# Key products of two blocks at once: the middle stage of a spectral attention kernel in turns of two blocks

## The chip, the cores and the metric

The kernel runs on one core of a Trainium2 chip. The metric is the device time of one execution in microseconds (us), from the first to the last instruction of the slowest core; here there is only one. The core has a matrix engine (PE), a vector engine (DVE), a scalar engine (ACT), a general engine (POOL) and a sync engine (SP) that here only issues transfers. Each engine works through its own program in order and waits on semaphores for the others.

## The reference

64 spectra `x` (256 degrees by 257 orders, complex) are turned into rows, then pass one attention layer and one small feed-forward layer:

```
coeff = complex(x) * sqrt_eig;  s = einsum('nlm,mlk->nkm', coeff, pct);  h = irfft(s, n=512)   # (64, 256, 512)
z = layernorm(h);  key = z @ K;  logits = tanh(key @ z.T + bias)
logits -= 10000 outside a band of 12;  scores = softmax(logits * temperature)
h = h + scores @ z
h = h + ffn(layernorm(h))     # 7 small layers, only on rows whose two marks are above 0.5; changes 32 columns
```

Layer norm has no weights, so the kernel applies its scale `rstd` afterwards. `K` and the transform are folded into one matrix `G`, so that keys come from the spectrum of a block and not from its rows. A block is one of the 64 items, 256 rows.

## The kernel before

There are three stages. The first (`stage1_spectrum`) multiplies the coefficients with `pct` and writes the spectra to DRAM; the last 12 groups of orders stay in an SBUF area called `hold` and are read from there for blocks 0 to 3 and stored to DRAM for the others (`store_held`, semaphore `hold_stored`). The middle stage (`stage2_blocks`) does transform, attention and output of all 64 blocks. The last stage runs the feed-forward layer on the marked rows.

Precision comes from splitting: each operand of a product is a high part (`sphi`, `keyhi`, `hhi`, `pThi`, rounded copies by ACT) and a low part (`splo`, `keylo`, `hlo`, `pTlo`, the rest by a subtraction on DVE), and `product3` (L668) issues three matmuls, high by high, high by low, low by high, per pair of 128 by 128 weights. For one block PE does:

- `keys` (L677): 4 output groups `e` of 4 depths of 3 matmuls, so 48 of 256 columns, weights `Ghi`/`Glo`, moving operand the block's spectrum, into two PSUM banks `ps_k`;
- `logits` (L722): 24 matmuls of 256 columns into `ps_l`;
- `probs_T`: 4 transposes of the probabilities into `ps_pT`; `rank`: 2 tiny ones; `inverse_dft`: 16 of 128 columns into `ps_dft`;
- `attend` (L733): 12 matmuls of 512 columns into `ps_av`.

ACT and DVE do the rest of a block: after the logits, DVE scales them (L1308), ACT takes tanh (L1057), DVE adds the band and finds the least (L1207), ACT takes the exponential (L989), PE transposes, ACT and DVE split (L1015, L1239). After `attend`, DVE adds the result to the rows (L1158, "mix"), ACT squares and sums (L953), POOL makes the root, ACT writes the output (L971). For a new block ACT copies the odd part of the transform (L1028), DVE makes the rows (L1274, L1286 to L1291), ACT squares and sums (L1049), and POOL makes `rstd`, which SP sends to DRAM and back as a row (`rrow`).

The stage is a software pipeline. Each engine has a function `slot(i, k, has)` that is its program for one slot, and `slots` (L550) runs i = -1 to 66. In slot i PE does, in this order, `keys(i)`, `probs_T(i-1)`, `rank(i-3)`, `inverse_dft(i+1)`, `logits(i)`, `attend(i-1)`. ACT copies `keyhi` in two halves around `sphi` of block i+1, DVE makes `keylo` likewise. At slot 59 (`LOOP[1]`) SP loads the constants of the last stage; at slot 60 (`WEIGHTS`) ACT and DVE round and split them (L980 to L981, `split_weights`) ahead of everything else of the slot. SP interleaves the stores of `hold` with the `rs` and `rrow` transfers of slots 0, 1 and 2:

```
if isinstance(i, int) and 0 <= i < 3:
    store_held(1 + 2 * i, min(3 + 2 * i, 6))
```

`sphi` and `splo` lie in an area of their own, two blocks deep, and are ready for slot i as soon as block i's spectrum is.

Of the kernel before, what the change touches and what calls it, by code (L numbers as in the profile page):

```python
# [17 lines left out]
P = 128  # L18
# [324 lines left out]
def stage2_blocks(nc, const, ffn_consts, spec, recs, rs, out):  # L343


    with ExitStack() as ctx:
# [16 lines left out]
        sb("early", [P, 10752])  # L363
# [9 lines left out]
        keyhi = place("keyhi", early_at + 38912, [P, CH, NLAT], F32R)  # L373
# [4 lines left out]
        held_at = const.hold_at  # L378
        act_f = place("act_f", held_at, [P, 2, TILES5, 512])
# [8 lines left out]
        y = place("y", held_at + 45568, [P, 512])  # L388

# [4 lines left out]
        keylo = sb("keylo", [P, CH, NLAT], F32R)  # L394
        rrow = sb("rrow", [P, 2, NLAT])
        lsc = sb("lsc", [P, TILES, NLAT])
        th = sb("th", [P, TILES, NLAT])
        lg = sb("lg", [P, TILES, NLAT])
# [33 lines left out]
        hot = sb("hot", [P, 2 * TJ, 16])  # L432
# [97 lines left out]
        FIRST, LAST = -1, NB + 2  # L530
        LOOP = (7, NB - 5)
# [18 lines left out]
        def slots(eng, slot):  # L550
            for i in range(FIRST, LOOP[0]):
                slot(i, i % 4, lambda n: 0 <= n < NB)
            with eng.Fori(LOOP[0], LOOP[1] - 3, 4) as i0:
                for u in range(4):
                    slot(i0 + u, (LOOP[0] + u) % 4, lambda n: True)
            for i in range(LOOP[1], LAST + 1):
                slot(i, i % 4, lambda n: 0 <= n < NB)
# [23 lines left out]
        def _(sp):  # L581
# [43 lines left out]
            def slot(i, k, has):  # L625
                if has(i):
                    sp.wait_ge(pool_rstd1, i + 1)
                    sp.dma_start(rs[i].rearrange("(p t) -> p t", p=P), rstd1[:, k, :]).then_inc(rs_written, 16)
                    wait(sp, dve_scaled, i - 1)
                    sp.wait_ge(rs_written, i * 16 + 16)  # L630
                    sp.dma_start(rrow[:, k % 2], rs[i].unsqueeze(0).to_broadcast([P, NLAT])).then_inc(rrow_loaded[k % 2], 16)
                if isinstance(i, int) and 0 <= i < 3:
                    store_held(1 + 2 * i, min(3 + 2 * i, 6))
                if isinstance(i, int) and i == 2:
                    sp.wait_ge(hold_stored, 16 * HELD)
                    for n in range(2):
                        sp.wait_ge(pe_dft, n * 2 + 2)
                        sp.wait_ge(act_sphi, n + 1)
                        sp.wait_ge(dve_splo, n + 1)
                        load(n + 4, n)  # L640
                if has(i) and has(i + 4) and not (isinstance(i, int) and i < 2):
                    sp.wait_ge(pe_dft, i * 2 + 2)
                    sp.wait_ge(act_sphi, i + 1)
                    sp.wait_ge(dve_splo, i + 1)
                    load(i + 4, k)
                if isinstance(i, int) and 2 <= i < 7:
                    empty_records((0, 1, 5, 9, 13)[i - 2], (1, 5, 9, 13, 16)[i - 2])
                if isinstance(i, int) and i == LOOP[1]:
                    for dst, src in ffn_consts:
                        sp.dma_start(dst, src).then_inc(ffn_loaded, 16)  # L650
                if isinstance(i, int) and i == AHEAD + 3:
                    for r in range(4):
                        sp.wait_ge(rec_sent[r], 32 * ((AHEAD - r + 3) // 4))
                    sp.wait_ge(rec_used, 1)
                    load_records(0, 0)
# [946 lines left out]
```

## Time and profile before

| | us |
|---|---|
| median of 3 runs (lowest to highest) | 1435.57 (1432.6 to 1438.91) |
| the profiled execution's own time | 1430.64 |
| its span, first to last instruction | 1428.6 |
| first stage, to the first matmul of the middle stage | about 325 |
| middle stage, to the last `attend` | about 325 to 1229 |
| last stage | about 1229 to 1428 |

Times in the rows below are microseconds from the start of the span. A timeline row gives start, duration, engine, line, operation, output and inputs, and a count; a bracket gives the idle time before it and who ended it. Matmuls are pipelined, so that a matmul's duration is longer than the distance between two starts; distances between starts are what counts on PE. On DVE and ACT the next instruction starts a little before the end of the one before.

### The profile page before, as it was taken

To read this page: it belongs to the slowest core of one execution; us is meant where nothing else is said; L and a number is where in the kernel's file an instruction comes from. 1 tells how busy PE (TensorE), PEld (TensorE's weight loads), DVE (VectorE), ACT (ScalarE), POOL (GpSimd) and SP (SyncE) were. 2 spreads that over 40 slices of the span, in tenths; PEclk is the share of its full clock that TensorE was granted. 3 is DMA by queue.
4 is the path that set the end of the run, shared out by engine and by line. 5 is a ranking of instruction groups with operands and counts; after the bars stand their busy time and mean duration, and the time that the engine had idled before them with its cause. 6 is when DMAs were issued, how large, how long until landed. Compare 5 with 4: busy or idle time off the path is not lost. (4 is left out here: it accounts for less than half of the span.)

```text
span 1428.6 us, 30500 instructions
## 1 busy us (share of the span) xinstructions
PE 1334.1 (93%) x8813; PEld 1158.9 (81%) x8813; DVE 929.4 (65%) x2026; ACT 899.9 (63%) x1956; POOL 559.5 (39%) x1394
## 2 busy tenths in 40 slices
PE   4999778798999999999999999999999989999994
PEld 3778666588899999999999999999999989545551
DVE  1232222235777878878788887888878878767772
ACT  1223222234677777777777777777777777867772
POOL 0000000000355555555555555555555546732222
PEclk8999999999999999999999999999999999999997
DMA  8999999994653433434334343343434332100000
GB/s 346 424 425 424 425 425 425 425 376 146 192 130 92 94 79 96 86 83 90 79 98 85 82 86 82 99 83 83 85 82 100 82 93 59 50 12 9 9 4 5
DMA packets 88315, 219.69 MB, mean 154 GB/s; under 512 B 20784, under 2 KB 33724, under 8 KB 75900
## 3 DMA queue, kind: packets, MB, share of 16 engines
q1 hardware_dynamic: 78728, 190.33, 42.8%
q10 hardware_dynamic: 4164, 27.27, 4.5%
q0 software_dynamic: 5376, 1.52, 0.6%
q8 instruction: 23, 0.38, 0.1%
q14 instruction: 24, 0.20, 0.1%
HBM read 147.77 MB, written 72.68 MB: 154 GB/s over the span
## 5 line engine op out<-in xcount | busy, mean ns | idle before, releaser
L674 PE MATMUL ps_k<-sphi,Glo 128*128 128x256 f32 x1024 | 292.2, 285 | 0.0
L673 PE MATMUL ps_k<-splo,Ghi 128*128 128x256 f32 x1024 | 291.0, 284 | 0.0
L672 PE MATMUL ps_k<-sphi,Ghi 128*128 128x256 f32 x1024 | 288.6, 282 | 0.0
L261 PE MATMUL s1b<-pg,cg 128*128 128x256 f32 x1024 | 240.5, 393 | 48.0 <-DVE cg L231 46.8
L261 PEld LDWEIGHTS s1b<-pg,cg 128*128 128x128 f32 x1024 | 198.0, 196 | 93.0 <-issue 33.9
L231 DVE TENSOR_TENSOR cg<-xg,se 128x1024 f32<-128x1024 f32 x63 | 77.2, 1225 | 221.5 <-DMA pg<-in_pct_dram 211.0
L1442 POOL TENSOR_SCALAR ve<-var 128x2 f32<-128x2 f32 x64 | 13.9, 217 | 479.8 <-ACT squares L1049 479.7
L672 PEld LDWEIGHTS ps_k<-sphi,Ghi 128*128 128x128 f32 x1024 | 194.7, 190 | 2.4
L673 PEld LDWEIGHTS ps_k<-splo,Ghi 128*128 128x128 f32 x1024 | 193.1, 189 | 2.7
L674 PEld LDWEIGHTS ps_k<-sphi,Glo 128*128 128x128 f32 x1024 | 193.7, 189 | 0.0
L316 ACT COPY stage<-s1b 128x512 f32<-128x512 f32 x104 | 60.7, 585 | 169.5 <-PE s1b L261 165.2
L1430 POOL DMA_INDIRECT recs<-rec,idx x128 | 136.9, 1069 | 54.6 <-issue 54.3
L672 PE MATMUL ps_l<-sphi,keyhi 128*128 128x256 f32 x512 | 150.9, 295 | 5.6 <-DVE keylo L1230 2.4
L673 PE MATMUL ps_l<-splo,keyhi 128*128 128x256 f32 x512 | 145.5, 284 | 0.0
L674 PE MATMUL ps_l<-sphi,keylo 128*128 128x256 f32 x512 | 145.4, 284 | 0.0
L708 PE MATMUL ps_dft<-dft,xt 128*128 128x129 f32 x1008 | 129.4, 282 | 0.0
L708 PEld LDWEIGHTS ps_dft<-dft,xt 128*128 128x128 f32 x1008 | 119.0, 194 | 0.0
L1049 ACT ACTIVATE squares<-h 128x512 bf16<-128x512 f32 x128 | 79.7, 624 | 56.6 <-DVE h L1291 56.6
L672 PEld LDWEIGHTS ps_l<-sphi,keyhi 128*128 128x128 f32 x512 | 98.7, 193 | 6.5 <-issue 5.3
L672 PE MATMUL ps_av<-hhi,pThi 128*128 128x512 f32 x256 | 100.5, 393 | 1.3 <-issue 1.3
L1218 DVE TENSOR_TENSOR keylo<-ps_k,keyhi 128x512 fp32r<-128x512 f32 x64 | 44.3, 692 | 86.8 <-ACT keyhi L999 86.8
L673 PE MATMUL ps_av<-hlo,pThi 128*128 128x512 f32 x256 | 100.4, 392 | 0.0
(175 smaller groups left out, 3181.0 us busy)
## 6 DMA issues: line engine op xcount, KB each, us to landing
pg<-in_pct_dram SPq DMA_DIRECT2D x63, 1024.0 KB, 25.7
out_dram<-o SPq DMA_DIRECT2D x64, 512.0 KB, 2.8
xg<-in_xs_dram SPq DMA_DIRECT2D x63, 512.0 KB, 24.2
xt<-spec SPq DMA_DIRECT2D x60, 512.0 KB, 5.2
spec<-stage ACTq DMA_DIRECT2D x52, 512.0 KB, 8.1
rrow<-rs SPq DMA_DIRECT2D x64, 128.0 KB, 4.6
spec<-hold SPq DMA_DIRECT2D x12, 480.0 KB, 5.2
recs<-rec SPq DMA_DIRECT2D x16, 160.0 KB, 5.6
```

The lines of the kernel that those rows point to most:

```text
L231: nc.vector.tensor_tensor(cg[:, b % SETS], xg[:, b], se_view(g), ALU.mult).then_inc(scaled, 1)
L261: last = nc.tensor.matmul(bank[at * PARTS + part][:, m % 2, :], cg[:, b % SETS, m * 2 + h, :], pg[:, b, m * 2 + h, :], start=(h == 0), sto ...
L316: nc.scalar.copy(to, bank[at * PARTS + j][:, :, :]).then_inc(copied, 1)
L672: nc.tensor.matmul(out_ap, whi, mhi, start=(j == 0), stop=False)
L673: nc.tensor.matmul(out_ap, whi, mlo, start=False, stop=False)
L674: last = nc.tensor.matmul(out_ap, wlo, mhi, start=False, stop=(j == n - 1))
L708: last = nc.tensor.matmul(ps_dft[t][:, cols[0]:cols[1]], x[:, src, t * P:(t + 1) * P], dft[:, cols[0]:cols[1]], start=True, stop=True)
L1049: nc.scalar.activation(squares[:, 0, t], h[:, k1, t], ACT.Square, scale=1.0 / math.sqrt(NLON), accum_out=var1[:, k1 % 2, t:t + 1]).then_in ...
L1218: nc.vector.tensor_tensor(keylo[:, 0:2, :].rearrange("p e w -> p (e w)"), ps_k[0][:, :], keyhi[:, 0:2, :].bitcast(F32).rearrange("p e w -> ...
L1430: nc.gpsimd.indirect_dma_start(out=recs[:, :], out_offset=bass.IndirectOffsetOnAxis(ap=idx[:, r4, t:t + 1], axis=0), in_=rec[:, r4, t, :], ...
L1442: nc.gpsimd.tensor_scalar(ve[:, 0, :], var1[:, k % 2, :], EPS, None, ALU.add).then_inc(pool_ve, 1)
```

## The change

The middle stage goes in turns of two blocks, a and a+1. `keys` now takes the spectra of both as one moving operand of 512 columns, so that a pair of blocks has 48 matmuls of 512 columns where it had 96 of 256. A group `e` fills one PSUM bank for both blocks, so that group 2 needs the bank of group 0 and group 3 that of group 1; the copies to `keyhi` and `keylo` are four per turn, one for each group. The spectra of a pair lie side by side, and there are two pairs; the second (`sphi1`, `splo1`) lies in the area `hold`. `lsc`, `th` and `lg` are dropped: the scaled logits, tanh, the band sum and the exponential are all written in place in `pr`. The program of each engine is rewritten for a turn. `exponentials` is L989, `squares1` L1049, `squares2` L953, `outputs` L971, `tangent` L1057, `odd_part` L1028, `rows_high` L1033, `spectrum_high` L1005; on DVE `least` is L1207, `mix` L1158, `rows_made` L1286 to L1291, `tail` the three small steps before the record, `even_odd` L1274, `scale_logits` L1308.

Places and bounds, and what SP does:

```diff
-        sphi = place("sphi", early_at + 16384, [P, 2, CH, NLAT], F32R)
-        splo = place("splo", early_at + 24576, [P, 2, CH, NLAT], F32R)
...
+        sphi = [place("sphi0", early_at + 16384, [P, CH, 2, NLAT], F32R),
+                place("sphi1", held_at, [P, CH, 2, NLAT], F32R)]
+        splo = [place("splo0", early_at + 24576, [P, CH, 2, NLAT], F32R),
+                place("splo1", held_at + 8192, [P, CH, 2, NLAT], F32R)]
...
-        LOOP = (7, NB - 5)
+        FIRST, LAST = -2, NB
+        LOOP = (6, NB - 6)
...
+                first = isinstance(a, int) and a == 0
...
+                if first:
+                    store_held(1, 3)
+                if has(a + 1):
+                    root_row(a + 1, r + 1)
+                if first:
+                    store_held(3, 6)
                     sp.wait_ge(hold_stored, 16 * HELD)
...
+                if has(a) and has(a + 4):
+                    load_behind(a, r)
...
+                if isinstance(a, int) and a == LOOP[1]:
                     for dst, src in ffn_consts:
                         sp.dma_start(dst, src).then_inc(ffn_loaded, 16)
...
+                if has(a + 2):
+                    root_row(a + 2, (r + 2) % 4)
```

PE, the keys and the order of a turn:

```diff
+            def keys(a, r):
+                pe.wait_ge(act_sphi, a + 2)
+                pe.wait_ge(dve_splo, a + 2)
+                for e in range(CH):
+                    wait(pe, act_keyhi, a * 2 + (e - 1 if e > 1 else 0))
+                    wait(pe, dve_keylo, a * 2 + (e - 1 if e > 1 else 0))
+                    product3(ps_k[e % 2][:, :],
+                             [(Ghi[:, d, e * P:(e + 1) * P], Glo[:, d, e * P:(e + 1) * P],
+                               sphi[r // 2][:, d].rearrange("p b w -> p (b w)"),
+                               splo[r // 2][:, d].rearrange("p b w -> p (b w)")) for d in range(CH)]).then_inc(pe_key, 1)
...
+                if has(a):
+                    keys(a, r)
...
+                if has(a - 1):
+                    probs_T(a - 1)
+                if has(a - 3):
+                    rank(a - 3, r + 1, a)
+                if has(a + 2):
+                    inverse_dft(a + 2, (r + 2) % 4)
+                if has(a):
+                    logits(a, r, a - 2)
+                if has(a - 1):
+                    attend(a - 1, (r + 3) % 4)
+                if has(a - 2) and not ending:
+                    rank(a - 2, r, a + 1)
+                if has(a + 3):
+                    inverse_dft(a + 3, (r + 3) % 4)
...
                     features_T(0)
+                if has(a):
+                    probs_T(a)
+                if has(a + 1):
+                    logits(a + 1, r + 1, a - 1)
+                if has(a):
+                    attend(a, r)
```

ACT, the high parts and the order of a turn:

```diff
+            def spectrum_high(n, r):
+                wait_spectrum(act, n, r)
+                if isinstance(n, int) and n == 2:
                     act.wait_ge(hold_stored, 16 * HELD)
...
+                    for q in (1, 3):
+                        act.wait_ge(x_loaded[q], 48)
+                wait(act, pe_logit, (n if r % 2 == 0 else n - 1) - 2)
+                nc.scalar.copy(sphi[r // 2][:, :, r % 2, :], spectrum_of(n, r)).then_inc(act_sphi, 1)
...
+                if isinstance(a, int) and a == WEIGHTS:
+                    weights()
+                if has(a - 1):
+                    exponentials(a - 1, (r + 3) % 4)
...
+                    squares2(a - 2, r % 2)
+                if has(a + 1):
+                    squares1(a + 1, r + 1)
+                if has(a):
+                    key_high(a, 0)
+                if has(a - 3) and not ending:
+                    outputs(a - 3, r + 1)
+                if has(a):
+                    key_high(a, 1)
+                if has(a + 2) and not start:
+                    spectrum_high(a + 2, (r + 2) % 4)
+                if has(a - 1) and not ending:
+                    rows_high(a - 1, (r + 3) % 4)
+                if has(a):
+                    key_high(a, 2)
+                if has(a + 3) and not start:
+                    spectrum_high(a + 3, (r + 3) % 4)
+                if has(a):
+                    key_high(a, 3)
+                if has(a - 1) and not ending:
+                    probs_high(a - 1, (r + 3) % 4)
+                if has(a - 3):
+                    places(a - 3, (r + 1) % 2)
+                if has(a + 2):
+                    odd_part(a + 2)
+                if has(a):
+                    rows_high(a, r)
...
+                    outputs(a - 2, r)
+                if has(a):
+                    tangent(a, r)
+                    exponentials(a, r)
+                if has(a + 2) and start:
+                    spectrum_high(a + 2, (r + 2) % 4)
+                    spectrum_high(a + 3, (r + 3) % 4)
+                if has(a - 2) and not ending:
+                    places(a - 2, r % 2)
+                if has(a + 3):
+                    odd_part(a + 3)
+                if isinstance(a, int) and a == NB - 2:
+                    round_in(0)
+                if has(a):
+                    probs_high(a, r)
+                if has(a - 1) and not ending:
+                    squares2(a - 1, (r + 1) % 2)
+                if has(a + 2):
+                    squares1(a + 2, (r + 2) % 4)
+                if has(a + 1):
+                    tangent(a + 1, r + 1)
```

DVE, the order of a turn:

```diff
+                if isinstance(a, int) and a == WEIGHTS:
+                    weights()
+                if has(a - 1):
+                    least(a - 1, (r + 3) % 4)
+                if has(a - 2):
+                    mix(a - 2, (r + 2) % 4)
+                if has(a + 1):
+                    rows_made(a + 1, r + 1)
+                if has(a):
+                    key_low(a, 0)
+                if has(a - 3):
+                    tail(a - 3, (r + 1) % 4)
+                if has(a):
+                    key_low(a, 1)
+                if has(a - 2) and not ending:
+                    tail(a - 2, (r + 2) % 4)
+                if has(a + 2) and not begin:
+                    spectrum_low(a + 2, (r + 2) % 4)
+                if has(a):
+                    key_low(a, 2)
+                if has(a - 1) and not ending:
+                    rows_low(a - 1, (r + 3) % 4)
+                if has(a):
+                    key_low(a, 3)
+                if has(a - 1):
+                    probs_low(a - 1, (r + 3) % 4)
...
+                if has(a + 2):
+                    even_odd(a + 2)
+                if has(a + 3) and not begin:
+                    spectrum_low(a + 3, (r + 3) % 4)
+                if has(a):
+                    scale_logits(a, r)
+                    least(a, r)
+                if has(a - 1) and not ending:
+                    mix(a - 1, (r + 3) % 4)
+                if has(a):
+                    rows_low(a, r)
+                if has(a + 2) and begin:
+                    spectrum_low(a + 2, (r + 2) % 4)
+                if has(a):
+                    probs_low(a, r)
+                if has(a + 2) and begin:
+                    spectrum_low(a + 3, (r + 3) % 4)
+                if has(a + 2):
+                    rows_made(a + 2, (r + 2) % 4)
+                if has(a + 1):
+                    scale_logits(a + 1, r + 1)
+                if has(a + 3):
+                    even_odd(a + 3)
+                if isinstance(a, int) and a == NB - 2:
+                    rows_low(a + 1, r + 1)
+                if ending:
+                    begin_step()
```

POOL does in a turn `root2(a-2)`, `root1(a+1)`, the marks, the record and the sending of block a-3, those of block a-2, `root2(a-1)`, `root1(a+2)`.

## Rows read from the trace of the kernel before

**Rows 1.** The page, its first part: busy time of each engine

```profile
PE 1334.1 (93%) x8813; PEld 1158.9 (81%) x8813; DVE 929.4 (65%) x2026; ACT 899.9 (63%) x1956; POOL 559.5 (39%) x1394
```

**Rows 2.** Windows, 600 to 900 us: busy time, instructions, clock, DMA

```profile
600.00:900.00 300.00, 300.00 (x2311) 288.84 (x2311) 244.60 (x566) 235.24 (x545) 172.00 (x456) 1.00 0.39 88
```

**Rows 3.** Timeline of PE, 800 to 815 us, where the product changes

```profile
800.82 0.40 PE L672 MATMUL ps_av<-hhi,pThi 128*128 128x512 f32 x1
...
803.57 0.29 PE L672 MATMUL ps_k<-sphi,Ghi 128*128 128x256 f32 x1
...
809.34 0.60 PE L696 MATMUL ps_pT<-ident,pr 128*128 128x128 f32 x4
809.78 0.17 PE L718 MATMUL ps_l<-mask,trib 128*128 128x3 bf16 x1
...
811.62 0.37 PE L672 MATMUL ps_l<-sphi,keyhi 128*128 128x256 f32 x1
...
814.58 0.40 PE L672 MATMUL ps_av<-hhi,pThi 128*128 128x512 f32 x1
```

**Rows 4.** Timeline of ACT, 803 to 816 us

```profile
803.43 1.09 ACT L1057 ACTIVATE th<-lsc,bias,rstd 128x256 f32<-128x256 f32 x2 [0.39 <-DVE lsc L1308]
...
806.14 0.63 ACT L953 ACTIVATE squares<-h 128x512 bf16<-128x512 f32 x1 [0.28 <-DVE h L1158]
...
807.39 0.56 ACT L999 CAST keyhi<-ps_k 128x512 fp32r<-128x512 f32 x1
...
810.02 0.84 ACT L1015 ACTIVATE pThi<-ps_pT,rstd 128x256 fp32r<-128x256 f32 x2
...
815.46 0.63 ACT L1049 ACTIVATE squares<-h 128x512 bf16<-128x512 f32 x1 [0.75 <-DVE h L1291]
```

**Rows 5.** Timeline of DVE, 804 to 815 us

```profile
804.16 0.48 DVE L1207 CUSTOM_DVE_ANT_0 lg<-th,band,ntemp 128x256 f32<-128x256 f32 x1 [0.77 <-issue]
...
805.28 1.41 DVE L1158 SCALAR_TENSOR_TENSOR h<-ps_av,rsum,h 128x512 f32<-128x512 f32 x2
808.05 0.69 DVE L1218 TENSOR_TENSOR keylo<-ps_k,keyhi 128x512 fp32r<-128x512 f32 x1 [1.37 <-ACT keyhi L999]
...
810.97 0.88 DVE L1239 SCALAR_TENSOR_TENSOR pTlo<-ps_pT,rstd,pThi 128x256 fp32r<-128x256 f32 x2
811.76 0.47 DVE L1175 TENSOR_SCALAR x<-h,rstd 128x128 f32<-128x128 f32 x2
...
814.07 0.68 DVE L1286 TENSOR_TENSOR h<-eo 128x508 f32<-128x508 f32 x1
```

**Rows 6.** Timeline, 349 to 351 us: PE starts again after DVE

```profile
349.45 0.68 DVE L1230 TENSOR_TENSOR keylo<-ps_k,keyhi 128x512 fp32r<-128x512 f32 x1
...
350.23 0.36 PE L672 MATMUL ps_l<-sphi,keyhi 128*128 128x256 f32 x1 [0.88 <-issue]
```

**Rows 7.** Timeline of SP's queue, 340 to 374 us: the stores of hold

```profile
340.97 5.56 SPq L599 DMA_DIRECT2D spec<-hold  x4
...
354.48 4.49 SPq L599 DMA_DIRECT2D spec<-hold  x4
...
366.69 0.88 SPq L599 DMA_DIRECT2D spec<-hold  x2
372.46 1.44 SPq L584 DMA_DIRECT2D xt<-spec  x3
```

**Rows 8.** Timeline, 1165 to 1176 us: the weights' slot, on DVE and PE

```profile
1165.73 0.68 DVE L1128 TENSOR_TENSOR W1r<-W1f,W1h 64x512 f32<-64x512 f32 x1 [4.58 <-ACT Whi L981]
...
1169.53 0.41 DVE L1207 CUSTOM_DVE_ANT_0 lg<-th,band,ntemp 128x256 f32<-128x256 f32 x1
...
1171.21 1.11 PE L696 MATMUL ps_pT<-ident,pr 128*128 128x128 f32 x4 [3.95 <-ACT pr L989]
...
1172.22 3.77 PE L708 MATMUL ps_dft<-dft,xt 128*128 128x129 f32 x16
```

**Rows 9.** Timeline of PE, 1226 us: the last block's attend

```profile
1226.38 0.47 PE L672 MATMUL ps_av<-hhi,pThi 128*128 128x512 f32 x1 [1.27 <-issue]
```

More of the change, by code:

```diff
@@ L662, in _ @@
+            turns(nc.sync, turn)
+            for n in (NB - 2, NB - 1):
+                store_out(n, n % 4)
             for r in range(4):
@@ L837, in body @@
                 for L in range(2, LAYERS):
-                    layer(s, L, between=(lambda: rank(NB - 1, (NB - 1) % 4)) if opening and L == 2 else None)
+                    layer(s, L, between=(lambda: rank(NB - 1, (NB - 1) % 4, NB)) if opening and L == 2 else None)
                     if L == LAYERS - 2 and not opening:
@@ new lines, in probs_high, with odd_part @@
+            def probs_high(n, r):
+                act.wait_ge(pe_pT, n + 1)
+                wait(act, pe_av, n * 2)
+                for t in range(TILES):
+                    nc.scalar.activation(pThi[:, t, :], ps_pT[:, t, :], ACT.Copy,
+                                         scale=rstd1[:, r, t:t + 1]).then_inc(act_pThi, 1)
+            def odd_part(n):
+                for t in range(TILES):
+                    act.wait_ge(pe_dft, n * 2 + t + 1)
+                    wait(act, dve_eo, (n - 1) * 4 + 2 * t + 2)
+                    nc.scalar.copy(od[:, t, :], ps_dft[t][:, HALF:NLON]).then_inc(act_od, 1)
@@ new lines, in rows_high, with squares1 @@
+            def rows_high(n, r):
+                act.wait_ge(dve_h, n * 3 + 3)
+                wait(act, pe_av, (n - 1) * 2)
+                nc.scalar.copy(hhi[:, r % 2], h[:, r]).then_inc(act_hhi, 1)
+            def squares1(n, r):
+                act.wait_ge(dve_h, n * 3 + 3)
+                wait(act, pool_rstd1, n - 1)
+                wait(act, act_var1, n * 2)
+                for t in range(TILES):
+                    nc.scalar.activation(squares[:, 0, t], h[:, r, t], ACT.Square, scale=1.0 / math.sqrt(NLON),
+                                         accum_out=var1[:, r % 2, t:t + 1]).then_inc(act_var1, 1)
@@ new lines, in weights, with least @@
+            def weights():
+                dve.wait_ge(hold_stored, 16 * HELD)
+                split_weights()
+                nc.vector.memset(feat[:, :, :], 0.0).then_inc(start, 1)
+                nc.vector.memset(res[:, :, :], 0.0).then_inc(rec_used, 1)
+            def least(n, r):
+                wait(dve, act_exp, n * 2)
+                for t in range(TILES):
+                    dve.wait_ge(act_tanh, n * 2 + t + 1)
+                    settled(dve)
+                    nc.vector.tensor_tensor_reduce(out=pr[:, t, :], in0=pr[:, t, :], in1=band[:, t, :],
+                                                   scale=ntemp[:, 0:1], scalar=HIGHEST, op0=ALU.add, op1=ALU.min,
+                                                   accum_out=nmx[:, r % 2, t:t + 1]).then_inc(dve_min, 1)
@@ new lines, in mix, with key_low @@
+            def mix(n, r):
+                sums(n, r % 2)
+                for t in range(TILES):
+                    mix_tile(n, (r + 2) % 4, t)
+            def key_low(a, e):
+                wait(dve, pe_logit, a)
+                dve.wait_ge(act_keyhi, a * 2 + e + 1)
+                nc.vector.tensor_tensor(
+                    keylo[:, e].rearrange("p b w -> p (b w)"), ps_k[e % 2][:, :],
+                    keyhi[:, e].bitcast(F32).rearrange("p b w -> p (b w)"), ALU.subtract).then_inc(dve_keylo, 1)
```

502 lines of the change are left out of this document (206 added, 296 removed).

## The prediction

> **What bounds the kernel now.** I read the page first: PE is busy 93% of the span [rows 1], but a matmul's duration says little, so the windows come next. From 600 to 900 us PE has no idle time at all and holds the full clock of 2.4 GHz, while DVE works 244.6 of 300 us and ACT 235.2 [rows 2]; the transfers take 39% of their engines. The middle stage is therefore set by PE's issue rate, and any edit must be priced by the distance between two matmul starts. The timeline of PE gives it: `keys` runs from 803.57 to 809.34, 5.77 us for 48 matmuls, so 120.2 ns for 256 columns; `attend` from 800.82 to 803.57, 2.75 us for 12, so 229.2 ns for 512 columns [rows 3]. The rest: four transposes 0.44, rank and transform 1.84, logits 2.96, attend 2.75. A block is 5.77 + 0.44 + 1.84 + 2.96 + 2.75 = 13.76 us, a pair 27.52.
>
> **The gain on PE.** A pair's keys become 48 x 229.2 ns = 11.00 us instead of 11.54: 0.54 us per turn, 16.7 over 31 turns, if PE stays dense. The bounds of the price: 227 ns (the smallest distance that rounding of the starts allows) and 240.4 (nothing gained, two times 256 columns). I take 229.2, because `attend` has the same shape, type and weights of 128 columns.
>
> On this point the Trainium skill (TensorE: Matmul & The Clock Gate, "Back-to-back issue gap") speaks against the change: start to start is N / 2.4 + 2.5 ns at the full clock, so 109.2 for 256 columns and 215.8 for 512, a gain of 2.6 ns per pair of matmuls and not 11.2, which would be 0.12 us per turn. The rows show 120.2 and 229.2, both larger than the rule, so I go by the rows.
>
> **Does PE stay dense?** Here the rewritten order decides. Group 2 of the keys needs the bank of group 0, so PE waits there for `key_low(a, 0)`. Before, no product of the keys waited for a copy of the same keys. Call P the moment at which `logits(a+1)` of the turn starts, behind `probs_T(a)`. PE reaches group 2 of the next turn 2.96 (logits) + 2.75 (attend) + 5.50 (groups 0 and 1) = 11.21 us after P. ACT and DVE, in their new order, must do a chain without a gap in the same time; each step is the distance between two starts in the rows of before:
>
> - transposes' end to `probs_high`: 810.02 against 809.34 + 0.60, and PE goes on at 809.78, so P + 0.20 (0.24 in the row, in which ACT comes out of a copy) [rows 3, 4]
> - `probs_high` to `probs_low` 0.95, `probs_low` to the next step of DVE, now `rows_made(a+2)`, 0.79 [rows 4, 5]
> - `rows_made` to `squares1(a+2)` 815.46 - 814.07 = 1.39 [rows 4, 5]
> - `squares1` to the next step, now `tangent(a+1)`: 1.24, by the like pair 806.14 to 807.39 [rows 4]; the scaled logits are there earlier, so that squares stand ahead of tanh
> - tanh to `least(a+1)` 0.73, `least` to `mix(a)` 1.12 [rows 4, 5]
> - `mix` to `rows_made(a+3)`: 1.33, its 1.41 less the overlap of 0.08 to 0.09 that 810.97 + 0.88 against 811.76 shows [rows 5]
> - `rows_made` to `squares1(a+3)` 1.39, `squares1` to `key_high(0)` 1.24 [rows 4, 5]
> - `key_high` to `key_low` 0.66, `key_low` 0.69 [rows 4, 5], and PE 0.10 later (349.45 + 0.68 to 350.23) [rows 6]
>
> The sum is 11.83, so PE arrives 0.62 us early, and its first matmul after a wait costs some 0.08 more (a matmul of 0.36 where 0.28 is usual) [rows 6]. The turn is then 15.75 (P back from group 2: 5.50 + 0.44 + 1.84 + 2.96 + 2.75 + 1.82 + 0.44) + 11.83 + 0.08 = 27.66 us, 0.14 more than the pair of before. Only half of the cheaper matmuls lie on this loop. ACT and DVE are no busier than before; what has changed is that squares of two new blocks and one tanh, least and mix stand in a row ahead of the copy that PE needs. Bounds: each of the 13 steps is read to 0.01 to 0.05, so the wait is 0.3 to 1.0; below 0 the price is -0.54 per turn. Behind the waiting PE stands its whole program. I went through the other waits of a turn in the same way, placing each engine's list on its own timeline; these are estimates: `key_low(1)` is done 1.0 us before group 3 needs it, `key_low(3)` 0.6 before `logits(a)`, `probs_T(a)` finds its exponential 1.2 early, POOL is ready with `root2(a-1)` 5 us early. The in-place tiles change no order, and SP's transfers keep their count. 30 turns, from the one at a = 2 to that at 62: +4.2 us.
>
> **The opening.** `sphi1` lies in `hold`, so `spectrum_high(2)` waits until all of `hold` is stored, and on ACT it stands ahead of `odd_part(3)` and `probs_high(0)`; `attend(0)` waits for those. Before, only SP waited for the stores. When are they done? The first group of four starts at 340.97 and the next at 354.48; the last two take 366.69 to 372.46, 5.77 us [rows 7]. In the new order the remaining six go together behind the row of block 1. Two more pairs at 3.0 to 4.3 each (a group of four less a round trip of some 3, less 5.77) make 13.0 for six. The start shifts little: block 0's rows now wait behind block 1's spectrum on ACT; 0 to 2 us, I take 0.6. Done: 354.48 + 0.6 + 13.0 = 368.1. Then on ACT two spectra of 0.95, odd part 0.55, `probs_high(0)`, and `probs_low(0)` 0.95 later: 371.5. From there DVE does 0.79, `splo` 1.14, and from `rows_made(2)` on the chain above (1.39 + 1.24 + 0.73 + 1.12 + 1.33 + 1.39 + 1.24 + 0.66 + 0.69 + 0.10 = 9.89): group 2 of turn 2 starts at 371.5 + 11.9 = 383.4. PE idles from about 358.5 (logits of block 1) to 372.5, and then runs `attend(0)` at 1.2 GHz, which the same chain hides. Bounds for the group's start: 376 (stores at the queue's best pace) to 388.
>
> **The weights' turn.** At 60 they still stand ahead of everything. The load no longer holds ACT up, since it is issued a turn of 27.7 us ahead. ACT needs some 1.8 for the two copies and DVE 3.80 (1165.73 to 1169.53) [rows 8]; `least(59)` shifts by 5.9, all of it behind a chain that is late already. PE idles 6.5 us and then runs at half the clock: that cost 0.51 in the transposes and 1.93 in the transform of before [rows 3, 8]. 5.9 + 2.4 = 8.3, where before lost 3.95 + 2.4 + 0.3 = 6.7.
>
> **The end.** From the turn at 62 (whose groups 0 and 1 end when group 2 starts, so its origin is 5.5 earlier): keys 11.0, transposes and rank 0.49, logits 2.96, attend 2.75, features 0.8, transposes 0.45, logits 2.96: 21.4. Then scale 0.9, tanh and `rows_high` 2.0, `rows_low` 1.1, `least` 0.6, exponential 1.2, transposes 0.5, split 2.1: `attend(63)` starts 29.9 after the origin.
>
> **The sum.** 383.4 + 0.1 + 30 x 27.66 = 1213.3; + 8.3 = 1221.6; - 5.5 + 29.9 = 1246.0 for `attend(63)`, which starts at 1226.4 before [rows 9]. The last stage is untouched. +19.6 us: +4.2 pace, +1.6 weights, about -1 the end, and the rest, near 15, the opening. The profiled execution took 1430.64 us, so 1450.2; it lies 4.9 under the median of the runs shown, so for the median 1455.
>
> **Rivals.**
>
> - *PE stays dense* (the other side). Place: group 2 of each turn. If one of the 13 steps is shorter than its row, or ACT and DVE have slack that I don't see, the turn is 26.98 and the 30 turns give -16.2 in place of +4.2: 1455 - 20.4 = 1435, no change. It decides for faster when the wait is gone and the opening costs under 8 us in place of 15: 1420 to 1428. For it speaks that DVE and ACT work only 82% and 78% of the time [rows 2]; against it, that the chain is strictly serial across both.
> - *The opening costs little.* The stores land by 360 us and PE goes on: some -10, so 1445 with the wait. Against it: the six stores alone cannot start before 354.5 [rows 7].
> - *The product of 512 columns saves nothing*, 240.4 ns: 24 matmuls on the loop, +0.27 per turn, 1463. By the rule of the Trainium skill named above it would be +0.21 per turn, 1461.
> - *More waits*: `key_low(3)` has 0.6 us of slack, and any further step in the turn that costs over 1 us puts 30 us on the whole: 1466 to 1490.
>
> **How the numbers follow.** Half for the forecast, its own range 1446 to 1463. The dense PE 0.24, split over same (0.11) and faster (0.13); the cheap opening 0.10, half of it within the bound; no saving 0.06; more waits 0.10. A change under 0.5%, 7 us, can't be told from none. Range 1432 to 1466: it leaves out the fast part of the dense case and the worse waits. Faster 0.13, same 0.17, slower 0.70.
>
> **What would show it.** In the profile of the changed kernel: keys of 512 columns 229 ns apart; PE idle 0.6 us once in each turn, ahead of `ps_k` and ended by DVE's `keylo`; turns of 27.7 us; PE idle 12 to 14 us near 360 and ACT's `sphi` waiting for `hold`; an idle of some 6.5 us at turn 60. The forecast is wrong if PE shows no idle at group 2 or if `attend(0)` starts before 365 us.

## The result and the profile after

The changed kernel takes 1477.37 us in the median of 4 runs (1476.65 to 1477.86) where the kernel before took 1435.19 beside it: a ratio of 1.029 [1.027, 1.032], 42 us slower. The forecast was 1455, the range ended at 1466. The direction and the place of the loss were right, its size was about half of what came. The profiled execution took 1477.86 us, its span 1476.1.

The page of the changed kernel, its first part and one line of its groups:

```profile
PE 1334.3 (90%) x7277; PEld 1072.1 (73%) x7277; DVE 933.8 (63%) x2026; ACT 899.2 (61%) x1956; POOL 601.4 (41%) x1394
...
L694 PE MATMUL ps_k<-sphi,Ghi 128*128 128x512 f32 x512 | 206.1, 403 | 29.6 <-DVE keylo L1305 29.6
```

1536 matmuls fewer than in [rows 1], and PE's busy time the same; new is an idle time of 29.6 us ahead of `ps_k`, 6.3 of it in the turn of the weights and the rest in 29 short waits. The windows of the same stretch as in [rows 2]:

```profile
600.00:900.00 300.00, 290.86 (x1728) 251.13 (x1727) 239.62 (x556) 229.23 (x533) 185.35 (x449) 1.00 0.33 80
```

PE is no longer dense: 9.1 us idle in 300. DVE and ACT did less in that stretch than before (239.6 and 229.2 against 244.6 and 235.2), so they had room; the clock stayed at its upper level. PE's timeline shows where the idle lies, always ahead of group 2 of the keys:

```profile
724.19 0.47 PE L694 MATMUL ps_k<-sphi,Ghi 128*128 128x512 f32 x1 [0.96 <-DVE keylo L1305]
...
729.84 0.60 PE L717 MATMUL ps_pT<-ident,pr 128*128 128x128 f32 x4
...
740.11 0.36 PE L694 MATMUL ps_l<-sphi,keyhi 128*128 128x256 f32 x1
...
752.24 0.47 PE L694 MATMUL ps_k<-sphi,Ghi 128*128 128x512 f32 x1 [0.68 <-DVE keylo L1305]
...
780.57 0.47 PE L694 MATMUL ps_k<-sphi,Ghi 128*128 128x512 f32 x1 [0.96 <-DVE keylo L1305]
```

Read as distances: 752.24 - 724.19 = 28.05 us for one turn, 780.57 - 752.24 = 28.33 for the next, and so on in alternation through the loop. Before it was 27.52 for the same two blocks, the forecast was 27.66. The idle is named by the wait that the prediction named.

From 740.11, the point P of the prediction, the chain on ACT and DVE can be followed to 752.24. ACT:

```profile
740.03 0.37 ACT L1052 COPY od<-ps_dft 128x256 f32<-128x256 f32 x1 [0.52 <-PE ps_dft L729]
740.39 0.84 ACT L1044 ACTIVATE pThi<-ps_pT,rstd 128x256 fp32r<-128x256 f32 x2
...
743.69 0.63 ACT L1066 ACTIVATE squares<-h 128x512 bf16<-128x512 f32 x1 [1.23 <-DVE h L1343]
...
744.94 1.08 ACT L1074 ACTIVATE pr<-pr,bias,rstd 128x256 f32<-128x256 f32 x2
...
749.49 0.63 ACT L1066 ACTIVATE squares<-h 128x512 bf16<-128x512 f32 x1 [0.51 <-DVE h L1343]
...
750.74 0.57 ACT L1027 CAST keyhi<-ps_k 128x512 fp32r<-128x512 f32 x1
```

and DVE:

```profile
741.34 0.88 DVE L1321 SCALAR_TENSOR_TENSOR pTlo<-ps_pT,rstd,pThi 128x256 fp32r<-128x256 f32 x2 [0.85 <-ACT pThi L1044]
742.13 0.68 DVE L1339 TENSOR_TENSOR h<-eo 128x508 f32<-128x508 f32 x1
...
743.32 0.33 DVE L1343 COPY h<-eo 128x8 f32<-128x8 f32 x1
...
745.66 0.48 DVE L1291 CUSTOM_DVE_ANT_0 pr<-pr,band,ntemp 128x256 f32<-128x256 f32 x1 [0.26 <-ACT pr L1074]
...
746.77 1.41 DVE L1243 SCALAR_TENSOR_TENSOR h<-ps_av,rsum,h 128x512 f32<-128x512 f32 x2
748.09 0.68 DVE L1339 TENSOR_TENSOR h<-eo 128x508 f32<-128x508 f32 x1
...
749.28 0.17 DVE L1343 COPY h<-eo 128x8 f32<-128x8 f32 x1
...
751.40 0.69 DVE L1305 TENSOR_TENSOR keylo<-ps_k,keyhi 128x512 fp32r<-128x512 f32 x1 [1.95 <-ACT keyhi L1027]
```

It is the forecast chain, link by link. Ten of the 13 steps differ by 0.02 us or less; three are longer. P to `probs_high` is 0.28 and not 0.20, since the copy `od` at 740.03 stands ahead of it; `rows_made` to `squares1(a+2)` is 1.56 and not 1.39 (the copy of 743.32 takes 0.33, like 27 of the 31 that have `scale_logits`, a reader of PSUM, directly behind them; the one of 749.28 takes 0.17, like all the others); `key_low` to PE is 0.84 and not 0.79. The chain has 12.13 us in place of 11.83.

The opening, with SP's queue, ACT and PE:

```profile
358.08 7.93 SPq L601 DMA_DIRECT2D spec<-hold  x6
...
370.35 1.99 ACT L1037 CAST sphi<-xt 128x1024 fp32r<-128x1024 f32 x2 [11.74 <-issue]
...
374.63 0.77 PE L694 MATMUL ps_av<-hhi,pThi 128*128 128x512 f32 x1 [12.44 <-ACT pThi L1044]
```

PE stands idle for 12.4 us (12 to 14 were forecast) and goes on when `hold` is stored. What comes next is not as forecast. The windows row of `attend(0)` (span, busy time of each engine, granted clock), then the `keylo` that group 2 of turn 2 needs, and the start of that group:

```profile
374.63:379.89 5.26, 5.26 (x12) 4.10 (x13) 5.17 (x14) 2.68 (x7) 0.94 (x2) 0.50 0.11 43
```

```profile
384.68 0.69 DVE L1305 TENSOR_TENSOR keylo<-ps_k,keyhi 128x512 fp32r<-128x512 f32 x1 [1.94 <-ACT keyhi L1027]
...
385.84 0.39 PE L694 MATMUL ps_k<-sphi,Ghi 128*128 128x512 f32 x1
```

`attend(0)` takes 5.26 us at a granted clock of 0.50, 1.2 GHz, where 2.75 are usual, and PE starts group 2 without an idle, some 0.5 us after `keylo` is done. Here the chain did not hide the slow clock; PE itself came last.

### The profile page after: what moved, and what is told of

Read it like the earlier page. It is cut to its first block, busy times and chain, and to the rows that moved or that the text cites. A ratio compares the mean times of both kernels' runs of the same rounds, so it can differ in the third digit from the quotient of the medians.

```text
span 1476.1 us, 27759 instructions
## 1 busy us (share of the span) xinstructions
PE 1334.3 (90%) x7277; PEld 1072.1 (73%) x7277; DVE 933.8 (63%) x2026; ACT 899.2 (61%) x1956; POOL 601.4 (41%) x1394
## 3 DMA queue, kind: packets, MB, share of 16 engines
q1 hardware_dynamic: 78728, 190.33, 39.7%
## 4 chain that ended last, share of the span: by engine, by line
PE 43%; DVE 12%; ACT 9%; issue 8%; POOL 1%; DMA 1%; ACTq 1%; SPq 1%; DVEq 0%; another core or an unknown queue 0%; POOLq 0%
PE ps_dft L729 8%; PE ps_k L694 5%; PE ps_k L695 4%; PE ps_k L696 4%; ACT squares L1066 3%; DVE h L1339 2%; DVE h L1341 2%; ACT pr L1074 2%; PE ps_l L694 2%; PE ps_l L696 2%; PE ps_l L695 2%; DVE h L1243 2%; PE ps_av L694 2%; PE ps_av L695 2%; PE ps_av L696 2%
## 5 line engine op out<-in xcount | busy, mean ns | idle before, releaser
L694 PE MATMUL ps_k<-sphi,Ghi 128*128 128x512 f32 x512 | 206.1, 403 | 29.6 <-DVE keylo L1305 29.6
L231 DVE TENSOR_TENSOR cg<-xg,se 128x1024 f32<-128x1024 f32 x63 | 77.2, 1226 | 225.9 <-DMA pg<-in_pct_dram 209.9
L695 PE MATMUL ps_k<-splo,Ghi 128*128 128x512 f32 x512 | 203.1, 397 | 0.0
L696 PE MATMUL ps_k<-sphi,Glo 128*128 128x512 f32 x512 | 202.8, 396 | 0.0
L1580 POOL TENSOR_SCALAR ve<-var 128x2 f32<-128x2 f32 x64 | 14.7, 229 | 383.8 <-ACT squares L1066 381.0
L1570 POOL DMA_INDIRECT recs<-rec,idx x128 | 151.9, 1187 | 46.2 <-issue 44.5
L1305 DVE TENSOR_TENSOR keylo<-ps_k,keyhi 128x512 fp32r<-128x512 f32 x128 | 88.3, 690 | 97.4 <-ACT keyhi L1027 94.6
L694 PEld LDWEIGHTS ps_k<-sphi,Ghi 128*128 128x128 f32 x512 | 97.2, 190 | 63.2 <-ACT keyhi L1027 41.8
L696 PEld LDWEIGHTS ps_k<-sphi,Glo 128*128 128x128 f32 x512 | 97.1, 190 | 23.1
L694 PE MATMUL ps_av<-hhi,pThi 128*128 128x512 f32 x256 | 102.3, 400 | 12.4 <-ACT pThi L1044 12.4
L695 PEld LDWEIGHTS ps_k<-splo,Ghi 128*128 128x128 f32 x512 | 97.4, 190 | 21.4
L1027 ACT CAST keyhi<-ps_k 128x512 fp32r<-128x512 f32 x128 | 74.0, 578 | 55.8 <-PE ps_k L696 54.2
```

Of the source, the lines that this page charges most:

```text
L231: nc.vector.tensor_tensor(cg[:, b % SETS], xg[:, b], se_view(g), ALU.mult).then_inc(scaled, 1)
L694: nc.tensor.matmul(out_ap, whi, mhi, start=(j == 0), stop=False)
L695: nc.tensor.matmul(out_ap, whi, mlo, start=False, stop=False)
L696: last = nc.tensor.matmul(out_ap, wlo, mhi, start=False, stop=(j == n - 1))
L1027: nc.scalar.copy(keyhi[:, e].rearrange("p b w -> p (b w)"), ps_k[e % 2][:, :]).then_inc(act_keyhi, 1)
L1305: nc.vector.tensor_tensor(keylo[:, e].rearrange("p b w -> p (b w)"), ps_k[e % 2][:, :], keyhi[:, e].bitcast(F32).rearrange("p b w -> p (b ...
```

## The experiments

All times of a run are read beside the kernel before on the same chip, so the ratio counts; medians of different runs are not to be compared. "Middle" is the distance on PE's timeline from the transposes that end the first stage to `attend(63)`; it leaves out the first stage, which differs by up to 3.7 us from one profiled run to the next, and the last. "Turn" is the distance of the same matmul in two turns of the loop.

| run | ratio to before | median us | middle us | turn us |
| --- | --- | --- | --- | --- |
| before | 1 | 1435.2 | 901.1 | 27.52 |
| changed | 1.029 [1.027, 1.032] | 1477.4 | 936.7 | 28.05 / 28.33 |
| e1 key copy first | 1.006 [1.004, 1.008] | 1437.9 | 904.8 | 27.12 |
| e2 products of 256 | 1.032 [1.030, 1.033] | 1474.4 | 939.7 | 28.17 / 28.45 |
| e3 spectra last in turn 0 | 1.026 [1.024, 1.027] | 1466.5 | 932.1 | 28.05 / 28.33 |
| e4 tanh before squares | 1.018 [1.016, 1.020] | 1455.7 | 923.7 | 27.61 / 27.80 |
| f0 changed, again | 1.029 [1.027, 1.032] | 1474.5 | 936.6 | 28.05 / 28.33 |
| f1 first stores only | 1.024 [1.021, 1.026] | 1466.6 | 925.6 | 28.05 / 28.33 |
| f2 e1 with products of 256 | 1.015 [1.012, 1.019] | 1454.7 | 914.1 | 27.51 |
| f3 e1 + f1 + weights | 0.995 [0.993, 0.997] | 1425.8 | 884.5 | 27.12 |
| g1 f3 + end order | 0.991 [0.989, 0.992] | 1422.2 | 885.5 | 27.12 |
| g2 loop of four turns | one run | 1499.1 | 960.0 | 28.05 / 33 to 34 |
| g3 weights in gaps | 1.022 [1.020, 1.025] | 1468.0 | 930.0 | 28.05 / 28.33 |
| g4 outputs before key copy | one run | 1548.4 | 1010.8 | 29.47 / 31.0 to 31.4 |

**f0: the changed kernel once more**, as a measure for the later runs.

> The changed kernel itself, once more, on the chip of the runs beside it, as their measure: 1.029 of the kernel before, all theories alike.

It repeats to 0.0003 of the ratio, and its middle to 0.1 us.

**e1: the first key copy ahead of the squares.** In ACT's turn:

```
-                if has(a + 1):
-                    squares1(a + 1, r + 1)
                 if has(a):
                     key_high(a, 0)
+                if has(a + 1):
+                    squares1(a + 1, r + 1)
```

> ACT copies the first key group (key_high(a,0)) ahead of squares1(a+1) instead of behind it. Serial chain theory: the steps rows_made, squares1 (1.40) and the copy's 1.25 no longer stand in a row; the copy starts some 1.7 us earlier, DVE is idle then, all waits of PE at group 2 (0.68 and 0.96 in turn) go, the turn falls from 28.19 to about 27.1, 28 turns and the one at the end give -30: 1447 us (1443 to 1452). Rival, ACT and DVE are simply too loaded in the new order: another wait takes the place (group 3, key_low(3) ahead of logits(a), or the exponentials) and the time stays within 7 us of 1477. Rival, contention: the single instructions stay longer than before and half of the gain comes, 1462.

Windows of this run:

```profile
600.00:900.00 300.00, 300.00 (x1812) 263.01 (x1811) 247.99 (x574) 236.90 (x554) 192.31 (x468) 1.00 0.34 88
```

PE is dense again, with one swap of two lines; the turn is 27.12 us and the middle 31.9 us shorter. No other wait took the place, and DVE and ACT work more per us than before the change without holding anyone up. Both rivals fall: it was order, not load. The turn gives PE's own price too: 27.12 without any idle, against 27.52 before, so the product of 512 columns is worth 0.40 us per turn. In the same rows 48 of them take 11.15 us, 232.3 ns each, 3 ns more than those of `attend`.

**e2 and f2: products of 256 columns, with the wait and without it.**

```
-                    product3(ps_k[e % 2][:, :],
...
+                    for q in range(2):
+                        last = product3(ps_k[e % 2][:, q * NLAT:(q + 1) * NLAT],
+                                        [(Ghi[:, d, e * P:(e + 1) * P], Glo[:, d, e * P:(e + 1) * P],
+                                          sphi[r // 2][:, d, q], splo[r // 2][:, d, q]) for d in range(CH)])
```

> The keys of a pair as 96 products of 256 columns again, order of all engines as in the changed kernel. Chain theory: only groups 2 and 3 lie on the loop that sets the turn (from group 2 to logits(a+1)); 24 products of 231 ns become 48 of 120.2, +0.2 to 0.25 per turn, so +6 to +7 us: 1484. Groups 0 and 1 grow into the wait of PE, which falls by 0.2 to 0.25. Rival, PE's issue sets the whole turn: +0.45 per turn, +14: 1491. Rival, the product of 512 columns saved nothing: 1477 and unchanged distance between the starts per column.

> The first key copy ahead of the squares (as in the run before of that kind, 1.006 of the kernel before), with products of 256 columns. There PE is dense, so this prices the product alone on the path: by the distances read (48 x 120.2 = 5.77 per block against 24 x 231 = 5.55) +0.43 us per turn of two blocks, turn 27.55 instead of 27.125, +13 us, 1.015 of the kernel before. Rival, the product of 512 columns saves nothing: 1.006, turn 27.1. Rival, ACT or DVE bind first: turn unchanged too, but with an idle of PE to be seen.

Under the wait, undoing the product costs 0.12 us per turn and 3 us in the middle, and PE's waits fall from 0.96 and 0.68 to 0.77 and 0.49: groups 0 and 1 grow into the wait. That is half of what was expected. The restart behind a wait costs 0.08 with 512 columns (the first distance is 0.31 where 0.23 is usual). With 256 the first distance is longer too, 0.19 where 0.12 is usual, but from group 2 to the transposes it is still 5.77 us, 48 x 120.2 ns, as without a wait. Without the wait, in f2 against e1, the same edit costs 0.38 per turn and 0.009 of the time, 13 us (9.3 in the middle), about as expected. The interval of e2's ratio and that of the changed kernel overlap, so its 3 us rest on the traces alone.

**e3 and f1: two ways around the wait for `hold`.** e3 moves the spectra of blocks 2 and 3 to the end of the first turn on ACT (as below) and likewise on DVE:

```
-                if has(a + 2) and start:
-                    spectrum_high(a + 2, (r + 2) % 4)
-                    spectrum_high(a + 3, (r + 3) % 4)
...
                 if has(a + 1):
                     tangent(a + 1, r + 1)
+                if has(a + 2) and start:
+                    spectrum_high(a + 2, (r + 2) % 4)
+                    spectrum_high(a + 3, (r + 3) % 4)
```

f1 leaves the order and cuts the wait down to the four stores that read what `sphi1` and `splo1` overwrite:

```
-                                     const.hold[c * NB + 4:c * NB + NB, 8 * j:8 * j + 8, :]).then_inc(hold_stored, 16)
+                                     const.hold[c * NB + 4:c * NB + NB, 8 * j:8 * j + 8, :]).then_inc(hold_first if j < 2 else hold_stored, 16)
...
-                    act.wait_ge(hold_stored, 16 * HELD)
+                    act.wait_ge(hold_first, 64)
```

> In the first turn the spectra of blocks 2 and 3, which need the stored hold, come last on ACT and DVE; probs_high(0), squares1(2) and tangent(1) go ahead of them. Theory: attend(0) starts near 362 instead of 374.6, keys(2) near 374 instead of 377.4, but least(1) to key_low(2,0) stand behind the second spectrum_low (about 373.6): group 2 of turn 2 at about 380.3 instead of 385.4, -5 us: 1472. Rival, the wait for the stores costs nothing of its own since the chain binds anyway: 1477 (0 to -1.5). Rival, the whole idle of 12.4 us is to be had by order alone: 1465.

> The changed kernel, but spectrum_high(2) waits only for the four stores that read the part of hold under sphi1 and splo1 (rows 0 to 15 of its 48), by a semaphore of their own, and not for all twelve. Theory of the prediction (the opening's loss is this wait): ACT goes on near 358 instead of 370, attend(0) starts near 362.5 instead of 374.6, group 2 of turn 2 near 373.5 instead of 385.4, and 12 us are gained: 0.8% below the changed kernel. Rival: the load of blocks 4 and 5 behind the last store (near 370) then holds back the transform of block 4 and half of the gain is lost, -6. Rival: nothing, since the chain of that turn binds anyway, 0.

e3 gained 4.6 us in the middle, f1 11.0, both close to the first theory. The timeline of f1:

```profile
358.53 1.98 ACT L1039 CAST sphi<-xt 128x1024 fp32r<-128x1024 f32 x2
...
362.80 0.47 PE L696 MATMUL ps_av<-hhi,pThi 128*128 128x512 f32 x1 [0.59 <-issue]
...
373.68 0.47 PE L696 MATMUL ps_k<-sphi,Ghi 128*128 128x512 f32 x1 [2.30 <-DVE keylo L1307]
```

The idle of 12.4 us ahead of `attend(0)` is 0.6, and 2.3 come back at group 2, where the chain is late. Behind that wait the granted clock of the next 5.6 us is 0.70. By the ratio the gain is 8 us and not 11, and the interval of each ratio, some 4 us to either side, allows both.

**e4: tanh ahead of the squares**, on ACT.

```
+                if has(a + 1):
+                    tangent(a + 1, r + 1)
                 if has(a + 2):
                     squares1(a + 2, (r + 2) % 4)
-                if has(a + 1):
-                    tangent(a + 1, r + 1)
```

> ACT does tangent(a+1) ahead of squares1(a+2). Chain theory: tanh can start when the logits are scaled (744.0 + 0.08) instead of behind the squares (744.94), so the chain is 0.86 shorter; the waits of 0.68 and 0.96 shrink to 0 and 0.1, turn 27.35 in the mean, -23 us: 1454 (1450 to 1460). Rival, squares1(a+2) later by 1.1 makes the row of block a+2 late on POOL and SP, and scale_logits(a+2) waits: 1477 or slower. Rival, the chain is not what PE waits for: 1477.

A miss in size: 13 us of 23. ACT does start the tanh 0.82 us earlier after `probs_high` (3.73 against 4.55), but DVE, its next link, is not free:

```profile
761.73 1.41 DVE L1331 TENSOR_TENSOR eo<-ps_dft,od 128x256 f32<-128x256 f32 x4
763.05 0.48 DVE L1291 CUSTOM_DVE_ANT_0 pr<-pr,band,ntemp 128x256 f32<-128x256 f32 x1
```

`even_odd(a+3)`, so far hidden, now stands on the chain, and `least` starts 1.20 behind the tanh in place of 0.72. About half of the 0.82 is left: the turns are 0.44 and 0.53 shorter, 27.61 and 27.80.

**g4: the chain made longer by a known step, with the same work.** On ACT:

```
+                if has(a - 3) and not ending:
+                    outputs(a - 3, r + 1)
                 if has(a):
                     key_high(a, 0)
-                if has(a - 3) and not ending:
-                    outputs(a - 3, r + 1)
```

> The changed kernel with outputs(a-3), 1.42 us of ACT, ahead of key_high(a,0) instead of behind it: the same work, the chain longer by 1.42. Serial chain theory: each of the 28 turns 1.40 longer (28.19 to 29.6), the wait of PE at group 2 of 0.8 becomes 2.2, +40 us: some 1515. Rival, the load of ACT and DVE sets the turn: the same work in another order, 1474 as before.

The load theory falls a second time. Each fourth turn is 29.47 us, 1.42 above 28.05, as the chain has it. The others cost 1.5 to 1.9 more than that, 0.28 of it the loop's end in every second turn; the rest I had not foreseen. PE's timeline and its windows (span, busy time of each engine, granted clock):

```profile
687.19 0.77 PE L694 MATMUL ps_k<-sphi,Ghi 128*128 128x512 f32 x1 [2.37 <-DVE keylo L1305]
...
718.07 0.47 PE L694 MATMUL ps_k<-sphi,Ghi 128*128 128x512 f32 x1 [2.09 <-DVE keylo L1305]
```

```profile
687.20:692.80 5.60, 5.60 (x18) 4.52 (x19) 4.19 (x13) 2.62 (x4) 3.87 (x15) 0.72 0.42 10
...
718.10:723.70 5.60, 5.60 (x24) 4.51 (x25) 5.46 (x14) 2.94 (x4) 4.53 (x14) 1.00 0.39 14
...
778.80:784.40 5.60, 5.56 (x17) 4.47 (x18) 4.14 (x13) 2.43 (x4) 3.75 (x15) 0.70 0.14 8
```

Behind the idle of 2.37 us PE ran a part of the next 5.6 us at 1.2 GHz (18 matmuls where there are 24 at the full clock); behind the one of 2.09 at 718 it did not, and behind one of the same length at 778.8 it did. Of the nine such waits in a row from 625 to 871 us, seven were followed by 5.6 us at 0.70 to 0.73 and two by 1.00; such a stretch has 6 or 7 matmuls of 0.23 us fewer, which is the 1.4 to 1.7 us. In the changed kernel, whose waits are below 1 us, the clock is 1.00 from 600 to 900 us.

**g2: four turns in the loop's body.** It asks why the turns alternate.

```
-        LOOP = (6, NB - 6)
+        LOOP = (6, NB - 10)
...
-            with eng.Fori(LOOP[0], LOOP[1] - 3, 4) as a0:
-                for u in (0, 2):
+            with eng.Fori(LOOP[0], LOOP[1] - 7, 8) as a0:
+                for u in (0, 2, 4, 6):
```

> The changed kernel with four turns in the loop's body (six passes over turns 6 to 52) in place of two. The turns alternate 28.05 and 28.33 there. Theory: the 0.28 is the loop's end on ACT and DVE, which falls between the squares or tanh of one turn and the exponentials and least of the next, in the middle of the chain: then three turns in a row take 28.05 and each fourth 28.33, the turns written out (54 to 58) 28.05; in all some -2 us. Rival: it comes from the parity of the pair (bank, buffer, queue): the alternation stays.

Three turns in a row take 28.05 and so do those written out behind the loop, so the 0.28 belongs to the loop's end, not to the parity of a bank or a queue. But each fourth turn takes 33 to 34 us, and the run is 25 us slower. The page's list of queues for the changed kernel has

```profile
q14 instruction: 25, 0.20, 0.1%
```

and for this run, with, under it, a line of its waits (us in all, times, longest):

```profile
q14 instruction: 109, 0.89, 0.4%
```

```profile
DVE pr L1291 <- issue: 21.0, 25, 2.0
```

Two of DVE's first instructions of a pass (`least`) wait 1.6 to 2.0 us each for nothing that the program orders, and four times as many instruction packets are moved. The likeliest reading is that the longer body is fetched again in each pass; that the fetch is the cause was not tried by itself.

**g3, f3 and g1: the weights, and all together.** g3 takes only the weights out of the way: `W1h` in turn 58, `Whi` in 60, and DVE's four operations in gaps of turns 60 and 62:

```
                 if has(a - 1) and not ending:
                     squares2(a - 1, (r + 1) % 2)
+                if isinstance(a, int) and a == WEIGHTS - 2:
+                    weights()
+                if isinstance(a, int) and a == WEIGHTS:
+                    weights2()
...
+                if isinstance(a, int) and a == WEIGHTS:
+                    weights()
+                if isinstance(a, int) and a == WEIGHTS + 2:
+                    split_weights3()
                 if has(a):
                     key_low(a, 1)
```

f3 joins this with e1 and f1. g1 changes the last turn as well, first on ACT, then on DVE:

```
                 if ending:
+                    outputs(a - 3, r + 1)
                     relu(0, 0, range(0, 2))
-                    outputs(a - 3, r + 1)
...
+                if ending:
+                    scaled_part(a - 3, (r + 1) % 2)
+                    rows_low(a - 1, (r + 3) % 4)
...
-                if isinstance(a, int) and a == NB - 2:
-                    rows_low(a + 1, r + 1)
```

> The changed kernel with the weights of the last stage in four pieces in the gaps of turns 58, 60 and 62, and nothing else. By the prediction's term (8.3 us for weights ahead of turn 60) and the 7.6 us that its turn is longer than the others: -7 to -8 us, 1.024 of the kernel before, PE's idle of 6.3 there back to 0.7. Rival: the pieces delay the chain, which is late in each of these turns, by their 3.8 us: -3 to -4.

> The first key copy ahead of the squares, the wait for the first four stores only, and the weights of the last stage rounded in four pieces over turns 58, 60 and 62, each in a gap of ACT or DVE, instead of all ahead of turn 60. Against the key copy alone (1.006 of the kernel before, 1437.9 us): -12 for the opening, -6 for the weights (PE idle of 4.4 and half-clock of some 2.4 gone, 0.8 lost to pieces longer than their gap): 0.993 to 0.995 of the kernel before, faster by 0.5 to 0.7%. Rival: a gain in one place is given back in another wait (the two are not additive), 1.000.

> The kernel with the key copy first, the wait for the first stores only and the weights in gaps (0.995 of the kernel before), and with its last turn reordered: least(63) ahead of rows_low(63), x2 of block 61 behind it and ahead of mix(62), outputs(61) ahead of the first relu. Theory: the last records are set out by POOL in one row from the mark of block 61 on, and the last stage's second step waits for them; POOL starts some 2 us earlier and no longer waits 2.8 us for the outputs of 61: -4 us, 0.992. attend(63) starts near 1206.3 where it was 1209.1. Rival: relu later by 1.4 us makes the first step of the last stage the bound, and nothing is gained: 0.995.

g3: middle 6.6 us shorter (7 to 8 expected), and PE's idle of 6.3 us there is 0.5. f3: 20.3 shorter than e1 (18 expected), so the two edits add up, and the kernel is 0.5% faster than before the change. g1: `attend(63)` did not come earlier (the middle is 1.0 longer: it waits 1.7 us for `pTlo`), but POOL sends its last records 29.7 us behind it in place of 32.7; 0.991 [0.989, 0.992], the fastest kernel of the study. f3 and g1 differ by 0.004 in ratio, 6 us, with intervals that do not meet, but only by 1.4 us in their traces behind the first stage, so how much the end order brings stays open.

## Why the prediction was wrong in size

Measured against its own sum: `attend(63)` was forecast at 1246.0 and started at 1265.1, and behind it 8.8 us were added where the prediction had none.

- *First stage*, +3.0. Its last transposes start at 328.34, and at 325.32 before. That part of the program is the same; f0, the same kernel, has 326.44.
- *Opening*, -0.7. Group 2 of turn 2 started at 385.8, 3.0 of that from the stage before; forecast 383.5. The stores were done at 370.3, so 367.3 without the shift (368.1 forecast). That the sum fits so well is in part luck: the slow `attend(0)`, which the chain was to hide, set this start, and the early stores made up for it. e3 and f1 show the wait to be the cause, and f1 that four of the twelve stores were enough to wait for.
- *The turn*, +14.7: the step that failed. "27.66 us, 0.14 more than the pair of before" was 28.19 in the mean over the 28 turns from 385.8 to 1175.0. Of the 0.53, the chain's three longer steps are 0.30; PE's own way back from group 2 to P is 15.93 in place of 15.83, mostly since keys of 512 columns cost 232.3 ns and not the 229.2 of `attend`; and 0.13 is the loop's end, 0.28 in every second turn of the loop, which the prediction did not have at all. The mechanism was right: e1 takes it away by order alone, g4 lengthens it by what is put into it. What made the size treacherous is that a wait is the small difference of two long sums, 11.83 and 11.21: 0.3 us read short in 13 steps of one is half as much again on the wait, times 28. The prediction's own bound for the wait, 1.0 us, would have given 30 x 0.38 = 11 us more, 1466: the range ended where this one term ended and had no room for the others.
- *Gain on PE*, 0.40 per turn and not 0.54, for the same 3 ns; it mattered little here, because most of it fell into the wait (e2); it counted in full once the wait was gone (f2). By the formula of the Trainium skill (TensorE: Matmul & The Clock Gate, "Back-to-back issue gap"), which that section gives for a single matmul, the gain would be 0.12 per turn. It had the direction of the miss; its two distances, 109.2 and 215.8 ns, are below both that were measured, 120.2 and 232.3 ns.
- *Weights*, +0.1: two turns took 63.7 us, forecast 63.6. Two errors meet here: the plain turn was longer than forecast, and the weights cost 7.6 us above it and not 8.3. g3 gives 6.6 of the 7.6 back.
- *The end*, +1.9 up to `attend(63)`: a wait of 2.3 us for the exponential and one of 1.9 us for POOL that the count of PE's work left out.
- *Last stage*, "untouched", +8.8. 4.1 are real: POOL sends its last records later behind `attend(63)`, since it waits for `outputs(61)`, which ACT does behind the first relu:

```profile
1268.54 0.24 POOL L1521 COPY rec<-o 128x64 f32<-128x64 f32 x1 [2.77 <-ACT o L1003]
```

  The other 4.7 are one stall in the last stage (a step of 39.7 us where its neighbours take 35.0) that nine of the fourteen profiled executions have, none of e1 to e4 and all of f0 to g4, and that the one of the kernel before happened not to have. The forecast had added 4.9 us for the distance of the profiled run from its median. By its size that covers the stall, which nothing in the working knew; so against 1455 the miss is 22 us, though the terms above miss by 28.

Two small slips in the working change nothing: the rows allow 2.74 / 12 = 228 ns as the smallest distance and not 227, and the terms of the end add up to 29.8 and not 29.9.

The rivals: *PE stays dense* needed an order that the change did not have; with it (e1) the time is 1.006 of before, 1444 on the scale of the forecast where the rival said 1435, the rest being PE's smaller gain and the last stage. *The product saves nothing* is refuted by f2 against e1, *the opening costs little* by `attend(0)` at 374.6. *More waits* had the right size for the wrong reason: `key_low(3)` held.

## What to carry to other kernels

When work is paired, ask what now stands in one row ahead of the first copy that frees a bank; a swap of two steps of one engine was worth 32 us here, and the product itself about 12. A wait forecast as a difference of two sums wants a range as wide as the reading error of all its steps, plus what the loop's end costs on each engine. Where a tile takes over space that is still being stored, wait for the stores of that space, not for all.

## What the runs showed that I had not expected

- A loop's end costs about 0.28 us on a chain that crosses it; twice the body did away with half of these and cost 5 to 6 us per pass instead, with 109 instruction packets in place of 25 (g2).
- Waits of 2.1 to 2.4 us, once a turn, brought the granted clock of the next 5.6 us to 0.70 to 0.73 in seven of nine in a row and left it at 1.00 in two; this nearly doubled the price of a step of 1.42 us (g4). Waits of 0.7 to 1.0 us cost nothing of the kind.
- The first matmul distance behind a wait was 0.31 us with 512 columns where 0.23 is usual; with 256 it was 0.19 where 0.12 is usual, but nothing of that was left in the sum of groups 2 and 3 (e2).
- A small copy on DVE (128x8) took 0.33 us in place of 0.17 in 27 of the 31 cases of the changed kernel in which `scale_logits` stood directly behind it, and never elsewhere; why was not tried.
- The same product shape ran at 229 ns in `attend` and at 232 in the keys; why was not tried.
